# Leaky relu of a graph attention layer: linear part by VectorE from PSUM instead of by a matmul

## The chip, the cores and the metric

One Trainium2 chip, one core. The metric is the device time of one execution in microseconds; the time shown for the kernel before is the median of three runs. The three layers share one program, launched once.

## What is computed

A small network on a graph of 3125 nodes with 32 features and 100000 edges (sorted by destination): an edge MLP, two graph convolutions, and then three attention layers (GATv2, 8 heads of 32 channels), with a layer norm behind each of the four. Only the attention layers matter here:

```python
xl = (x @ Wl).reshape(-1, H, C)
xr = (x @ Wr).reshape(-1, H, C)
e = jax.nn.leaky_relu(xl[src] + xr[dst], 0.2)
logits = jnp.einsum('ehc,hc->eh', e, att)
m = jax.ops.segment_max(logits, dst, num_segments=N_NODES)
p = jnp.exp(logits - m[dst])
denom = jax.ops.segment_sum(p, dst, num_segments=N_NODES)
alpha = p / denom[dst]
out = jax.ops.segment_sum(alpha[:, :, None] * xl[src], dst, num_segments=N_NODES)
return out.mean(axis=1) + bias
```

Since leaky_relu(z) = 0.2 z + 0.8 relu(z), its sum with `att` can be made in two parts: a linear one, straight from the rows x of an edge's two nodes, and one from relu(z).

## The kernel before, in words

Edges lie in slots of 128, one edge to a partition; 8 slots make one step g (512 columns by 2 sides), there are G = 104 steps a layer, and 8 steps make a chunk. A loop over u = 0 to G + LAG - 1 (LAG = 10) runs on every engine, each with its own written-out list of instructions in fixed order; semaphores tie them. In step u the rows of step u are turned into logits, while step k = u - 10 is weighted and summed into `acc`.

- GpSimd, `pool_gathers` (L340): 8 indirect DMAs for each g, fetching table rows into one of two `rows` buffers. It waits until TensorE (`x_made`) and ScalarE (`xs_kept`) are done with g - 2.
- TensorE, `pe_attention`: `z_half(u,0)` (L848) multiplies the turned rows `xT` by `wcat` into two PSUM banks Z; `sums_half(k,0)` (L877) sums weighted rows; `linear(u)` (L856) adds the linear part of the logits into bank LG by way of `linblk`; `z_half(u,1)` writes the same two banks Z once more; `logits_half(u,0)` (L865) multiplies relu(z) by `attblk`; `rows_in(u+1)` (L833, L836) turns the next rows; `sums_half(k,1)`; `logits_half(u,1)`. Before `z_half` it waits on `rz_made`, since the banks must have been read.
- ScalarE, `act_attention`: `leaky(g,t)` (L573) makes relu(z) of two banks into `rz`; further it copies rows and logits, and takes exponentials.
- VectorE, `attention(l)`: `weigh(k,side)` (L1432), weights times rows, 1056 elements, one operand in PSUM; `add(k,side)` (L1442), twice, into `acc` at a window read from a register. At a chunk's end, where phase = u % 8: phase 0 has two scans (L1445, L1449) and `exchange` (L1457 to L1470), whose result TensorE turns (L920) before it ends the step; phase 1 has `settle`, with two scans again, `lasts`, `fall`; phase 2 has `fscale` (L1037), which waits for a small matmul of TensorE (L894), and a scaling of `acc` (L1498) ahead of all else. VectorE works through its list strictly in order.

The weights' preparation stands in the first convolution's setup (L1374 to L1382): `linblk` and the last columns of `wcat` are made there by products with `att`, reduces and copies.

The wait that the change touches most, on TensorE:

```python
def z_half(g, t):
    pe.wait_ge(xt_ready, l * G + g + 1)
    pe.wait_ge(rz_made, 4 * (l * G + g) + 2 * t)
```

Of the kernel before, what the change touches and what calls it, by code (L numbers as in the profile page):

```python
# [17 lines left out]
ALU = mybir.AluOpType  # L18
# [7 lines left out]
P = 128  # L26
# [42 lines left out]
def build(nc, x, edge_blocks, L0, W_gcn, b_gcn, gat, out):  # L69
    with ExitStack() as ctx:  # L70
# [58 lines left out]
        linblk = [sb(f"linblk{l}", [P, 7 * H + P]) for l in range(LAYERS)]  # L129
# [123 lines left out]
        rz_made, l_summed, lg_copied = sem("rz_made"), sem("l_summed"), sem("lg_copied")  # L253
# [305 lines left out]
        def act_attention(act, l):  # L559
# [8 lines left out]
            def leaky(g, t):  # L568
# [3 lines left out]
                for side in range(2):  # L572
                    act.activation(rz[:, 2 * t + side, :], ps[:, Z + side, :], ACT.Relu).then_inc(rz_made, 1)  # L573
# [66 lines left out]
        def _(act):  # L640
            act.wait_ge(weights_zeroed, 2 + 3 * LAYERS)
# [179 lines left out]
        def pe_attention(pe, l):  # L821
# [21 lines left out]
            def z_half(g, t):  # L843
                pe.wait_ge(xt_ready, l * G + g + 1)
                pe.wait_ge(rz_made, 4 * (l * G + g) + 2 * t)
# [5 lines left out]
            def linear(g):  # L851

                n = g % 8
                if n == 0:
                    pe.wait_ge(lg_copied, l * CHUNKS + g // 8)
                pe.matmul(ps[:, LG, :], linblk[l][:, (7 - n) * H:(7 - n) * H + P], xT[:, g % 2, :],  # L856
                          start=(n == 0), stop=False, skip_group_check=True)

            def logits_half(g, t):
                n = g % 8  # L860
                pe.wait_ge(rz_made, 4 * (l * G + g) + 2 * t + 2)
                for side in range(2):
# [3 lines left out]
                              start=False, stop=(n % 4 == 3 and t == 1), skip_group_check=True).then_inc(l_summed, 1)  # L866
# [16 lines left out]
            for u in range(G + LAG):  # L883
# [11 lines left out]
                if u < G:  # L895
                    linear(u)
                    z_half(u, 1)
                    logits_half(u, 0)
# [125 lines left out]
        def _(v):  # L1024
# [80 lines left out]
            for t in [w1[:, :], w2[:, :, :]] + [w[:, :, :] for w in wcat] + [w[:, :, :] for w in attblk] + [w[:, :] for w in linblk]:  # L1105
                v.memset(t, 0.0).then_inc(weights_zeroed, 1)
# [111 lines left out]
            for l in range(LAYERS):  # L1218
                ts(attblk[l][:, :, 3 * H:4 * H], attblk[l][:, :, 3 * H:4 * H], 0.8, None, ALU.mult)
# [149 lines left out]
            tmp2 = T2f[:, 0:2 * HC].rearrange("p (k c) -> p k c", k=2)  # L1369
            tmp = T2f[0:C, 2 * HC:3 * HC]  # L1370
            for l in range(LAYERS):


                stt(tmp2, wcat[l][:, :, 0:HC], 0.2, down(attrow[l][:, :], 2), ALU.mult, ALU.mult)  # L1374
                for k in range(2):
                    link(v.tensor_reduce(wcat[l][:, k, HC:ZC], tmp2[:, k, :].rearrange("p (h c) -> p h c", h=H),
                                         AX.X, ALU.add))
# [258 lines left out]
```

## Time and profile before

| | |
|---|---|
| median of 3 runs | 6472.8 us (6467.22 to 6487.99) |
| the profiled execution's own time | 6470.45 us |
| its span | 6468.7 us |
| mean granted TensorE clock | 0.92 |
| busy: TensorE, weight load | 84%, 55% |
| busy: GpSimd, VectorE, ScalarE | 65%, 50%, 30% |

Busy time is the time in which an engine had an instruction running, as a share of the span. TensorE's matmuls are pipelined, and one float32 matmul of the program is two records (so `z_half`, two matmuls, is x4); from the start of one to the start of the next instruction is the better measure of what it costs. The three attention loops lie at 2767 to 3904, 4006 to 5150 and 5252 to 6392 us.

### The profile page before, as it was taken

Reading aid. Unit: us, or ns where it says so; the run is one execution under the profiler, and the core shown is the slowest. Engines: PE = TensorE matmul, PEld = TensorE weight load, DVE = VectorE, ACT = ScalarE, POOL = GpSimd, SP = SyncE. Lnnn points to the kernel's source line nnn. Section 1 sums busy time; section 2 is a strip of 40 time slices with the busy share of each in tenths; the row PEclk is TensorE's granted clock in tenths of the full one; section 3 lists DMA queues with packets and bytes.
Section 4 is the critical chain, followed back from the end, with each engine's and each line's share of the span. In section 5 each row is a group of like instructions: output and inputs, shape, how many; then the busy total and the mean of one; then the engine's idle time right before and its main releaser. Section 6 shows DMA issues by size and latency. Waiting matters only on the chain.

```text
span 6468.7 us, 138175 instructions
## 1 busy us (share of the span) xinstructions
PE 5462.8 (84%) x47565; PEld 3535.7 (55%) x47565; DVE 3216.3 (50%) x5767; ACT 1959.8 (30%) x3916; POOL 4227.3 (65%) x4383
## 2 busy tenths in 40 slices
PE   1888888868886888689999986899999679999995
PEld 1666666667775777535455544354444444455553
DVE  8222323266567555535555555355555624555555
ACT  0333334345551000033333321333333123333330
POOL 0777777657775777477777742777777147777770
PEclk8899989879997999789999996999999879999997
DMA  1444444323332332234444431444444224444441
GB/s 36 113 114 113 113 113 113 102 72 83 78 83 66 83 83 77 54 87 119 117 121 121 120 94 38 104 120 117 121 121 118 65 56 116 120 119 121 119 117 32
DMA packets 645340, 626.97 MB, mean 97 GB/s; under 512 B 366244, under 2 KB 447915, under 8 KB 644779
## 3 DMA queue, kind: packets, MB, share of 16 engines
q1 hardware_dynamic: 498218, 437.16, 22.1%
q0 software_dynamic: 140352, 181.29, 14.6%
q8 instruction: 312, 5.11, 0.3%
q10 hardware_dynamic: 6208, 1.37, 0.1%
q14 instruction: 250, 2.04, 0.1%
HBM read 530.77 MB, written 88.55 MB: 96 GB/s over the span
## 4 chain that ended last, share of the span: by engine, by line
PE 40%; POOL 29%; issue 15%; DVE 9%; ACT 2%; DMA 2%; DVEq 1%; POOLq 0%
POOL rows L340 29%; PE ps L761 11%; PE ps L877 10%; PE ps L848 4%; PE ps L776 4%; PE ps L865 2%; PE ps L856 2%; DMA rows<-table,idx 2%; DVE region L1326 1%; DVE acc L1442 1%; PE ps L947 1%; PE ps L833 1%; PE ps L788 1%; DVE region L1034 1%; PE ps L963 1%
## 5 line engine op out<-in xcount | busy, mean ns | idle before, releaser
L340 POOL DMA_INDIRECT rows<-table,idx x3328 | 3231.9, 971 | 1556.8 <-issue 1108.3
L877 PE MATMUL ps<-region,hot 128*128 128x272 f32 x4992 | 1320.0, 408 | 92.2 <-DVE acc L1442 87.9
L877 PEld LDWEIGHTS ps<-region,hot 128*128 128x128 f32 x4992 | 910.9, 192 | 507.9 <-issue 335.8
L573 ACT ACTIVATE region<-ps 128x512 f32<-128x512 f32 x1248 | 677.4, 595 | 1681.9 <-PE ps L848 1681.9
L1442 DVE TENSOR_TENSOR acc<-acc,ps 128x272 f32 x1248 | 545.2, 437 | 1195.6 <-PE ps L877 1088.5
L1432 DVE TENSOR_TENSOR region<-ps,region 128x1056 f32<-128x1056 f32 x624 | 781.7, 1253 | 64.8 <-issue 53.7
L761 PE MATMUL ps<-hot,region 128*128 128x192 bf16 (+1 forms) x7488 | 773.0, 266 | 13.2 <-issue 9.6
L848 PE MATMUL ps<-xT,wcat 64*128 64x512 f32 x2496 | 721.9, 655 | 7.4 <-ACT region L573 4.9
L761 PEld LDWEIGHTS ps<-hot,region 128*128 128x128 bf16 x7488 | 701.9, 105 | 40.8 <-issue 9.9
L352 POOL DMA_INDIRECT rows<-table,idx x528 | 502.6, 952 | 270.5 <-issue 160.3
L865 PE MATMUL ps<-region,attblk 128*32 128x512 f32 x2496 | 667.5, 614 | 0.0
L352 POOL DMA_INDIRECT region<-table,idx x512 | 487.2, 952 | 156.0 <-issue 156.0
L848 PEld LDWEIGHTS ps<-xT,wcat 64*128 64x128 f32 x2496 | 193.4, 189 | 463.8 <-issue 431.0
L1289 DVE TENSOR_TENSOR acc<-acc,ps 128x96 f32 (+1 forms) x832 | 252.2, 303 | 354.4 <-PE ps L788 127.5
L833 PEld LDWEIGHTS ps<-identb,rows 128*32 128x32 bf16 x7488 | 239.8, 97 | 270.5 <-issue 264.5
L833 PE MATMUL ps<-identb,rows 128*32 128x128 bf16 x7488 | 300.0, 223 | 93.1 <-DMA rows<-table,idx 89.4
L620 ACT ACTIVATE region<-iota,region 128x128 bf16<-128x128 f32 x832 | 254.2, 389 | 283.3 <-PE ps L796 270.9
L856 PE MATMUL ps<-xT,linblk 128*128 128x512 f32 x624 | 331.3, 613 | 0.0
L836 PE MATMUL ps<-turned,xwin 128*32 128x128 bf16 x7488 | 313.2, 223 | 0.0
L1231 DVE TENSOR_TENSOR region<-ps,b3row 128x512 f32<-128x512 f32 x104 | 71.9, 691 | 483.5 <-PE ps L725 483.5
L776 PE MATMUL ps<-region 128*128 128x224 f32 x1248 | 308.3, 371 | 0.0
L1309 DVE TENSOR_TENSOR region<-ps,gmask 128x448 f32<-128x448 f32 x312 | 193.8, 621 | 176.8 <-PE ps L761 176.0
(264 smaller groups left out, 5880.0 us busy)
## 6 DMA issues: line engine op xcount, KB each, us to landing
hot<-hot_dram SPq DMA_DIRECT2D x624, 256.0 KB
turned<-turned_dram SPq DMA_DIRECT2D x624, 128.0 KB
rows<-table,idx POOLq DMA_INDIRECT x3856
hot_dram<-hot SPq DMA_DIRECT2D x104, 512.0 KB
xwin<-table SPq DMA_DIRECT2D x1664, 24.0 KB
region<-hot_dram SPq DMA_DIRECT2D x78, 512.0 KB
turned_dram<-turned SPq DMA_DIRECT2D x104, 256.0 KB
region<-r_dram SPq DMA_DIRECT2D x78, 256.0 KB
```

Of the source, the lines that this page charges most:

```text
L340: pool.indirect_dma_start(rows[:, b, j, :], None, table, bass.IndirectOffsetOnAxis(ap=idx[:, s:s + 1], axis=0)).then_inc(gathered[b], 16)
L352: pool.indirect_dma_start(rows4[at % 4][:, j, :], None, table, bass.IndirectOffsetOnAxis(ap=idx[:, 8 * g + j:8 * g + j + 1], axis=0)).then ...
L573: act.activation(rz[:, 2 * t + side, :], ps[:, Z + side, :], ACT.Relu).then_inc(rz_made, 1)
L761: mm = pe.matmul(ps[:, GB + i % 2, 224 * j:224 * j + n], bt[b][:, k, at:at + P], tabparts[:, k::FOLD, (2 + s) * C:(3 + s) * C], start=(k = ...
L776: mm = pe.matmul(ps[:, DB[i % 2], 0:GROUPS * C], dhot[b][:, at, :], picked[b][:, at, :, :].rearrange("p g c -> p (g c)"), start=(j == 0), ...
L833: m1 = pe.matmul(ps[q:q + C, XT, j * P:(j + 1) * P], rowparts[b][:, at, 2 * C + s * C:2 * C + (s + 1) * C], identb[:, :], start=(s == 0), ...
L848: pe.matmul(ps[:, Z + side, :], wcat[l][q:q + 64, side, t * P:(t + 1) * P], xT[q:q + 64, g % 2, :], start=True, stop=True).then_inc(z_summ ...
L856: pe.matmul(ps[:, LG, :], linblk[l][:, (7 - n) * H:(7 - n) * H + P], xT[:, g % 2, :], start=(n == 0), stop=False, skip_group_check=True)
L865: pe.matmul(ps[q:q + 32, LG, :], attblk[l][:, t, p_:p_ + 4 * H], rz[:, 2 * t + side, :], start=False, stop=(n % 4 == 3 and t == 1), skip_g ...
L877: mm = pe.matmul(ps[:, AG + i, 0:PC + H], hot[:, b, 4 * side + 2 * i + j, :], px[b][:, 4 * side + 2 * i + j, :], start=(j == 0), stop=(j = ...
L1432: v.tensor_tensor(to, at.unsqueeze(3).broadcast_to([P, 4, H, HK]), xs[:, (k // 8) % 2, n, 4 * side:4 * side + 4, :].unsqueeze(2).broadcast ...
L1442: v.tensor_tensor(at, at, ps[:, AG + i, 0:PC + H], ALU.add).then_inc(att_added, 1)
```

## The change

The linear matmul, `linblk` and the preparation for both go. ScalarE's Relu now carries the factor 0.8 and counts on a semaphore of its own, `relu_made`. TensorE's `z_half` and `logits_half` wait for that. There are two of the new instructions in each of the 104 steps of each layer. The gathers stay as they are.

```diff
-        linblk = [sb(f"linblk{l}", [P, 7 * H + P]) for l in range(LAYERS)]
...
-                    act.activation(rz[:, 2 * t + side, :], ps[:, Z + side, :], ACT.Relu).then_inc(rz_made, 1)
+                    act.activation(rz[:, 2 * t + side, :], ps[:, Z + side, :], ACT.Relu, scale=0.8).then_inc(relu_made, 1)
...
             def z_half(g, t):
                 pe.wait_ge(xt_ready, l * G + g + 1)
-                pe.wait_ge(rz_made, 4 * (l * G + g) + 2 * t)
+                pe.wait_ge(rz_made, 2 * (l * G + g) + t)
...
-            def linear(g):
-
-                n = g % 8
-                if n == 0:
-                    pe.wait_ge(lg_copied, l * CHUNKS + g // 8)
-                pe.matmul(ps[:, LG, :], linblk[l][:, (7 - n) * H:(7 - n) * H + P], xT[:, g % 2, :],
-                          start=(n == 0), stop=False, skip_group_check=True)
-
             def logits_half(g, t):
                 n = g % 8
-                pe.wait_ge(rz_made, 4 * (l * G + g) + 2 * t + 2)
+                pe.wait_ge(rz_made, 2 * (l * G + g) + t + 1)
+                if n == 0 and t == 0:
+                    pe.wait_ge(lg_copied, l * CHUNKS + g // 8)
...
                 if u < G:
-                    linear(u)
                     z_half(u, 1)
...
-            for l in range(LAYERS):
-                ts(attblk[l][:, :, 3 * H:4 * H], attblk[l][:, :, 3 * H:4 * H], 0.8, None, ALU.mult)
...
-                stt(tmp2, wcat[l][:, :, 0:HC], 0.2, down(attrow[l][:, :], 2), ALU.mult, ALU.mult)
-                for k in range(2):
-                    link(v.tensor_reduce(wcat[l][:, k, HC:ZC], tmp2[:, k, :].rearrange("p (h c) -> p h c", h=H),
-                                         AX.X, ALU.add))
-                    cp(linblk[l][:, 7 * H + 64 * k:8 * H + 64 * k], wcat[l][:, k, HC:ZC])
...
+                def leaky(g, t):
+                    if g >= G:
+                        return
+                    v.wait_ge(relu_made, 4 * (l * G + g) + 2 * t + 2)
+                    to = rz[:, 2 * t:2 * t + 2, :]
+                    v.scalar_tensor_tensor(to, ps[:, Z:Z + 2, :], 0.2, to, ALU.mult, ALU.add).then_inc(rz_made, 1)
...
                     link(scan_ahead(c, carrycol[:, 0:1]))
+                    leaky(u, 0)
                     link(scan_back(c, carrycol[:, 1:2]))
...
                         if k + 1 >= 0 and k + 1 < G:
                             weigh(k + 1, 0)
+                        leaky(u, 0)
                         v.wait_ge(lg_copied, l * CHUNKS + c + 1)
...
                             weigh(k + 1, 1)
+                        leaky(u, 1)
                         exchange(c)
...
                         if windows:
                             add(k, 0, windows)
+                        leaky(u, 1)
                         v.wait_ge(fall_made, l * CHUNKS + c + 1)
...
                         if 0 <= k + 1 < G:
                             weigh(k + 1, 0)
+                        leaky(u, 0)
+                        if 0 <= k + 1 < G:
+                            weigh(k + 1, 1)
                         if windows:
                             add(k, 0, windows)
-                        if 0 <= k + 1 < G:
-                            weigh(k + 1, 1)
+                        leaky(u, 1)
                         if windows:
                             add(k, 1, windows)
```

How the instructions stand, at three places. In these rows `region` is one of three large buffers that hold `rz`, weights and scans; a scan is shown as SCALAR_TENSOR_TENSOR too, told by its line and by `newF` or `newR`.

VectorE, phase 0 of a chunk, before, from the first `weigh` to the second:

```order
L1432 TENSOR_TENSOR region<-ps,region 128x4x264
L1445 SCALAR_TENSOR_TENSOR region<-newF,region 128x512
L1449 SCALAR_TENSOR_TENSOR region<-newR,region 128x512
L1442 REGISTER_ALU
L1442 ISA
L1442 TENSOR_TENSOR acc<-acc,ps 128x272
L1442 REGISTER_ALU x2
L1442 ISA
L1442 TENSOR_TENSOR acc<-acc,ps 128x272
L1432 TENSOR_TENSOR region<-ps,region 128x4x264
```

The same place in the changed kernel, from behind the first `weigh` to the exchange's first copy (L1423 is `weigh`, L1413 the new `leaky`, L1436 and L1440 the scans, L1433 `add`, L1035 a copy):

```order
L1413 SCALAR_TENSOR_TENSOR region<-ps,region 128x1024
L1436 SCALAR_TENSOR_TENSOR region<-newF,region 128x512
L1440 SCALAR_TENSOR_TENSOR region<-newR,region 128x512
L1433 REGISTER_ALU
L1433 ISA
L1433 TENSOR_TENSOR acc<-acc,ps 128x272
L1433 REGISTER_ALU x2
L1433 ISA
L1433 TENSOR_TENSOR acc<-acc,ps 128x272
L1423 TENSOR_TENSOR region<-ps,region 128x4x264
L1413 SCALAR_TENSOR_TENSOR region<-ps,region 128x1024
L1035 COPY ahead<-ps 1x16x16
```

`leaky(u,0)` stands ahead of the scans, `leaky(u,1)` between the second `weigh` and the exchange.

VectorE, phase 2, before, from `fscale` on:

```order
L1037 TENSOR_SCALAR fscale<-ps,first_hot 128x8
L1421 TENSOR_LOAD packed
L1421 ISA x2
L1498 REGISTER_ALU
L1498 ISA
L1498 TENSOR_TENSOR acc<-acc,fscale 128x264
L1432 TENSOR_TENSOR region<-ps,region 128x4x264
```

and in the changed kernel:

```order
L1029 TENSOR_SCALAR fscale<-ps,first_hot 128x8
L1405 TENSOR_LOAD packed
L1405 ISA x2
L1490 REGISTER_ALU
L1490 ISA
L1490 TENSOR_TENSOR acc<-acc,fscale 128x264
L1423 TENSOR_TENSOR region<-ps,region 128x4x264
L1413 SCALAR_TENSOR_TENSOR region<-ps,region 128x1024
L1423 TENSOR_TENSOR region<-ps,region 128x4x264
L1433 TENSOR_TENSOR acc<-acc,ps 128x272
```

The new instruction stands behind `fscale`, the scaling of `acc` (L1490) and the first `weigh`; the second `weigh` is now ahead of the adds.

TensorE, the start of the same phase 2, before:

```order
L924 MATMUL ps<-ident,region 128x128 x4
L848 MATMUL ps<-xT,wcat 128x512 x2
L877 MATMUL ps<-region,hot 128x272 x4
L894 MATMUL ps<-fdiag,ones 128x8
L856 MATMUL ps<-xT,linblk 128x512
L848 MATMUL ps<-xT,wcat 128x512 x2
L865 MATMUL ps<-region,attblk 32x512 x2
```

and in the changed kernel (L847 `z_half`, L870 `sums_half`, L887 the small matmul, L858 `logits_half`):

```order
L916 MATMUL ps<-ident,region 128x128 x4
L847 MATMUL ps<-xT,wcat 128x512 x2
L870 MATMUL ps<-region,hot 128x272 x4
L887 MATMUL ps<-fdiag,ones 128x8
L847 MATMUL ps<-xT,wcat 128x512 x2
L858 MATMUL ps<-region,attblk 32x512 x2
```

The linear matmul between the small one and the second `z_half` is gone.

## Rows read from the trace of the kernel before

**Rows 1.** First loop: window, us, busy (x) of PE PEld DVE ACT POOL, clock, DMA.
```profile
2767.00:3904.00 1137.00, 1064.83 (x8686) 538.18 (x8686) 572.78 (x880) 361.96 (x781) 779.16 (x816) 0.98 0.43 111
```

**Rows 2.** The gathers' line in that loop: durations in ns, and waits.
```profile
L340 POOL DMA_INDIRECT rows<-table,idx x816: 938/944/1938, 2766.7 to 3808.5; - x164
...
  PE ps L836: 7.3, 2
```

**Rows 3.** TensorE in time order, ordinary step u = 22: start us, us, instruction.
```profile
2986.97 1.13 PE L848 MATMUL ps<-xT,wcat 64*128 64x512 f32 x4
...
2989.97 1.02 PE L856 MATMUL ps<-xT,linblk 128*128 128x512 f32 x2
2990.92 1.13 PE L848 MATMUL ps<-xT,wcat 64*128 64x512 f32 x4
...
2993.64 2.10 PE L877 MATMUL ps<-region,hot 128*128 128x272 f32 x8
...
2996.65 1.13 PE L848 MATMUL ps<-xT,wcat 64*128 64x512 f32 x4
```

**Rows 4.** ScalarE in time order, same step: the two Relus.
```profile
2988.18 1.08 ACT L573 ACTIVATE region<-ps 128x512 f32<-128x512 f32 x2 [3.29 <-PE ps L848]
```

**Rows 5.** A VectorE line in the convolutions, 1024 elements, one input in PSUM.
```profile
L1326 DVE TENSOR_TENSOR region<-dloc,ps x130: 1211/1214/1221, 1350.5 to 2673.8; 128x1024 bf16<-128x1024 f32 x130
```

**Rows 6.** VectorE in time order, steps u = 22 and 24 to 26.
```profile
2987.03 1.26 DVE L1432 TENSOR_TENSOR region<-ps,region 128x1056 f32<-128x1056 f32 x1 [0.23 <-issue]
...
3008.56 1.22 DVE L1445 TENSOR_TENSOR_SCAN region<-newF,region 128x512 f32<-128x512 bf16 x1
...
3012.08 1.25 DVE L1432 TENSOR_TENSOR region<-ps,region 128x1056 f32<-128x1056 f32 x1
3014.64 0.41 DVE L1043 COPY ahead<-ps 1x256 f32<-1x256 f32 x1 [1.31 <-PE ps L905]
...
3017.27 0.16 DVE L1043 COPY ahead<-state 1x8 f32<-1x8 f32 x1
...
3024.97 0.44 DVE L1442 TENSOR_TENSOR acc<-acc,ps 128x272 f32 x1 [0.36 <-DVE acc L1442]
...
3034.19 1.26 DVE L1432 TENSOR_TENSOR region<-ps,region 128x1056 f32<-128x1056 f32 x1
```

**Rows 7.** TensorE in time order: first `z_half` of steps 8, 24 to 27, 103; one `sums_half`.
```profile
2839.72 1.13 PE L848 MATMUL ps<-xT,wcat 64*128 64x512 f32 x4
...
3007.35 1.13 PE L848 MATMUL ps<-xT,wcat 64*128 64x512 f32 x4
...
3017.76 1.13 PE L848 MATMUL ps<-xT,wcat 64*128 64x512 f32 x4
...
3025.56 2.07 PE L877 MATMUL ps<-region,hot 128*128 128x272 f32 x8
...
3029.13 1.13 PE L848 MATMUL ps<-xT,wcat 64*128 64x512 f32 x4
...
3039.73 0.70 PE L848 MATMUL ps<-xT,wcat 64*128 64x512 f32 x2
...
3815.66 0.70 PE L848 MATMUL ps<-xT,wcat 64*128 64x512 f32 x2
```

**Rows 8.** A pause of TensorE in the third loop, and the granted clock behind it.
```profile
5408.55 0.22 PE L833 MATMUL ps<-identb,rows 128*32 128x128 bf16 x1 [1.87 <-DMA rows<-table,idx]
...
5409.33 3.56 PE L877 MATMUL ps<-region,hot 128*128 128x272 f32 x8
5412.83 0.80 PE L865 MATMUL ps<-region,attblk 128*32 128x512 f32 x2
...
5409.90:5413.20 3.30, 3.30 (x9) 1.88 (x9) 0.44 (x2) 0.22 (x1) 2.64 (x3) 0.50 0.20 37
```

**Rows 9.** GpSimd in time order: a gather beside a scan of phase 1.
```profile
3019.63 1.66 POOL L340 DMA_INDIRECT rows<-table,idx  x1 [0.30 <-issue]
```

**Rows 10.** A group of the setup that the change removes.
```profile
L1376 DVE TENSOR_REDUCE wcat<-T 128x8 f32<-128x256 f32 x6 | 2.5, 420 | 0.2
```

More of the change, by code:

```diff
@@ L252, in build @@
         x_made, xt_ready, xs_kept = sem("x_made"), sem("xt_ready"), sem("xs_kept")
-        rz_made, l_summed, lg_copied = sem("rz_made"), sem("l_summed"), sem("lg_copied")
+        rz_made, relu_made, l_summed, lg_copied = sem("rz_made"), sem("relu_made"), sem("l_summed"), sem("lg_copied")
         heads_made, tails_turned = sem("heads_made"), sem("tails_turned")
@@ L640, in _ @@
         def _(act):
-            act.wait_ge(weights_zeroed, 2 + 3 * LAYERS)
+            act.wait_ge(weights_zeroed, 2 + 2 * LAYERS)
             for dst, srcw in weights:
@@ L865, in logits_half @@
                     pe.matmul(ps[q:q + 32, LG, :], attblk[l][:, t, p_:p_ + 4 * H], rz[:, 2 * t + side, :],
-                              start=False, stop=(n % 4 == 3 and t == 1), skip_group_check=True).then_inc(l_summed, 1)
+                              start=(n % 4 == 0 and t == 0), stop=(n % 4 == 3 and t == 1), skip_group_check=True).then_inc(l_summed, 1)
             def sums_half(k, side):
@@ L1103, in add_steps @@
                         between[k]()
-            for t in [w1[:, :], w2[:, :, :]] + [w[:, :, :] for w in wcat] + [w[:, :, :] for w in attblk] + [w[:, :] for w in linblk]:
+            for t in [w1[:, :], w2[:, :, :]] + [w[:, :, :] for w in wcat] + [w[:, :, :] for w in attblk]:
                 v.memset(t, 0.0).then_inc(weights_zeroed, 1)
@@ L1368, in _ @@
             T2f = T2[:, :, :].rearrange("p w c -> p (w c)")
-            tmp2 = T2f[:, 0:2 * HC].rearrange("p (k c) -> p k c", k=2)
             tmp = T2f[0:C, 2 * HC:3 * HC]
             for l in range(LAYERS):
-                stt(tmp2, wcat[l][:, :, 0:HC], 0.2, down(attrow[l][:, :], 2), ALU.mult, ALU.mult)
-                for k in range(2):
-                    link(v.tensor_reduce(wcat[l][:, k, HC:ZC], tmp2[:, k, :].rearrange("p (h c) -> p h c", h=H),
-                                         AX.X, ALU.add))
-                    cp(linblk[l][:, 7 * H + 64 * k:8 * H + 64 * k], wcat[l][:, k, HC:ZC])
                 tt(wsum[l][:, 0:HC], wsum[l][:, 0:HC], wcat[l][0:C, 0, 0:HC], ALU.add)
@@ L1471, in exchange, with settle @@
                     v.sem_inc(carry_made, 1)
-                def settle(c):
+                def settle(c, u):
                     at = l * CHUNKS + c
@@ L1484, in settle @@
                     v.tensor_scalar(fall[:, :], fall[:, :], 0.0, first_old[0:H, c:c + 1], ALU.min, ALU.mult).then_inc(e_made, 1)
-                for u in range(8, G + LAG):
+                for u in range(G + LAG):
                     phase, c, k = u % 8, u // 8 - 1, u - LAG
@@ L1489, in attention @@
                     if phase == 1 and ends:
-                        settle(c)
+                        settle(c, u)
                     if phase == 2 and ends and c > 0:
```

## The prediction

> **What bounds the kernel now.** The page first: TensorE 84% busy, GpSimd 65%, VectorE 50%. Such shares are means over stages, so the second view is the stretch of one attention layer's loop, the only place (with a short setup) that the change touches. There TensorE is busy for 1064.8 of 1137 us and GpSimd for 779.2, VectorE for 572.8 [rows 1], and one would say that TensorE bounds the loop and that a matmul less must help. The third view, the gather's own line, speaks against it: its 816 gathers run from 2766.7 to 3808.5, which is 10.2 us for each step of eight, and of all that time GpSimd waited 7.3 us for TensorE [rows 2]. So the gathers hold the loop, and TensorE keeps up with a little to spare. How little is read from its timeline: an ordinary step goes from 2986.97 to 2996.65, 9.68 us [rows 3]. The three steps at a chunk's end, where VectorE's scans and the exchange lie between TensorE's parts, take longer: phase 0 from 3007.35 to 3017.76 is 10.41, phase 1 to 3029.13 is 11.37, phase 2 to 3039.73 is 10.60 [rows 7]. Eight steps of TensorE's own chain are 5 x 9.68 + 32.38 = 80.8 us, while eight steps in truth take 82.2 (from u = 8 at 2839.72 to u = 103 at 3815.66 are 95 steps in 975.9 us, 10.27 each [rows 7]). The chain has 1.4 us in 82 to spare: less cannot be gained there, since every gather stays, and a chain that grows by more is paid in full.
>
> **What is removed.** The linear matmul holds TensorE from 2989.97 to 2990.92, 0.95 us a step [rows 3]. By itself that would shorten a chain that does not bound: worth nothing but at the loop's last step. In the setup the products, the six reduces (0.42 each [rows 10]) and the copies of `linblk` go; with products and small copies I put the piece at 2.0 us a layer, 6 us in all. TensorE waits for VectorE there, so the 6 us are gained (lower end 0).
>
> **What is added, ordinary step.** Two new VectorE instructions, 1024 elements from PSUM and SBUF. The nearest row, 1024 elements with one PSUM input, took 1.21 us, and the `weigh` with 1056 took 1.26 [rows 5, 6]; I take 1.22. 312 x 2 x 1.22 = 761 us of VectorE time, and it has room: the question is what waits. Times are from the start of `z_half(u,0)`. The Relu runs from 1.21 to 2.29 [rows 4]. The second `z_half` used to need only that, and came at 3.95 after sums and linear [rows 3]; now it also needs `leaky(u,0)`. VectorE is free (its `weigh` ran 0.06 to 1.32 [rows 6]). With 0.10 for the handover from ScalarE (no row shows it; between 0 and the 0.15 that VectorE to TensorE takes, 3025.41 to 3025.56 [rows 6, 7]) it runs 2.39 to 3.61, and `z_half(u,1)` starts at 3.76. Without linear TensorE was ready at 3.00, so it idles 0.76. From there to the next step are 5.73 us as before (2990.92 to 2996.65), and `leaky(u,1)`, done some 3.76 later, is hidden behind rows and sums. The step: 3.76 + 5.73 = **9.49**, 0.19 less than now. Four fifths of the saved matmul are lost to the wait.
>
> **Phase 0.** The scans began 1.21 into the step [rows 6]; they now stand behind `leaky(u,0)` and begin at 3.54 (successive instructions overlap by some 0.07), a shift of 2.33. The second `weigh` ended at 5.98, now at 8.31. Then `leaky(u,1)`, to 9.45, and only then the exchange, which used to begin at 7.29 and takes 2.79 (3014.64 to 3017.43 [rows 6]). It ends at 12.17. TensorE needs its result before it ends the step, 0.33 later: **12.50** instead of 10.41.
>
> **Phase 1.** `settle` has `leaky(u,0)` between its two scans: all behind it comes 1.14 later, the second `add` ends at 7.65 + 1.14 = 8.79 [rows 6]. `sums_half(k,1)` waits for it, and so it did before, so the whole 1.14 shows: 11.37 becomes **12.51**.
>
> **Phase 2** is where the order hurts most. `fscale` and the scaling of `acc` wait for a matmul and stand first, then the `weigh` from 5.06 to 6.32 [rows 6], then `leaky(u,0)`: 6.24 to 7.46. `z_half(u,1)` is ready near 3.4 and starts at 7.61, and 5.73 follow: **13.34** instead of 10.60. TensorE pauses some 4 us.
>
> **The sum.** Eight steps: 5 x 9.49 + 12.50 + 12.51 + 13.34 = 85.8 us against 82.2. The gathers (two buffers of rows) no longer decide. Over the 95 steps: 12 x 12.50 + 12 x 12.51 + 11 x 13.34 (the first chunk has no `fscale`) + 60 x 9.49 = 1016, against 975.9: +40.3 a layer. *The clock:* at 5408.55 TensorE had paused 1.87 us; behind it the granted clock was 0.50, the 1.2 GHz level, for 3.3 us, and a `sums_half` that takes 2.03 to the next instruction took 3.50 [rows 3, 8]. The pause of 4 us in phase 2 should do this each time, and TensorE is the chain just then: 11 x 1.6 = +17.6 a layer (ends 0 and three times that). *The tail:* in six steps behind the last row step both `weigh` now stand ahead of the adds; between 0 and 1.25 us each, I take 0.87 since TensorE has nothing else left there, 5.2, less one linear 0.95: +4.3. Three layers: 3 x (40.3 + 17.6 + 4.3) = 186.6, less 6 for the setup: **+181 us**. Against the profiled execution's 6470.45 this is 6651; the median of the runs shown, 6472.8, is 2 us above that execution, which changes nothing at this size.
>
> **A rule against the change, on the gathers.** The rows: a gather beside the scan of phase 1, two SBUF inputs, took 1.66 us instead of the median 0.944 [rows 2, 9]; yet with two `weigh` in each step (one input in PSUM) the median stays there. `leaky` has one PSUM input too, so I add nothing. The Trainium skill, page "SBUF — State Buffer", section "SBUF: two separate sides", says that a VectorE instruction in a two-port mode or with two SBUF inputs can lock GpSimd out of the port pair they share, and warns that this starves gathers issued by GpSimd. By its exact wording `leaky` is exempt; by its warning taken broadly the third rival below would come out.
>
> **The rivals.**
> 1. *The clock does not fall.* For it: over the loop the mean is 0.98 [rows 1], pauses and all. Then 6651 - 53 = **6598**.
> 2. *The clock falls more.* Phase 0 has a pause too, about 1.7 us before the exchange's end, and a pause of 4 us could cost twice. 3 x (17.6 + 12 x 1.6) = +110: **6761**.
> 3. *Gathers are held up by `leaky`.* Each for its 1.22: 8 gathers then take 9.99 + 2.44 = 12.4 us, 2.2 above 10.27, over 312 steps +675: some **7140**. The `weigh` rows speak against it.
> 4. *The other side: not slower.* The gathers stay the bound, because VectorE reaches its `leaky` sooner in the three chunk-end steps than I lay out (its adds and `weigh` overlapping the waits). The point that decides: eight steps of the chain at or under 82.2 us, so the three may lose only 2.4 together where I have 6.0. Then only the setup is gained: 6470 - 6 = **6464**. Against it: three separate places, each with the order fixed in one in-order queue.
>
> **How the numbers follow.** Forecast 0.50, clock does not fall 0.22, clock falls more 0.18, not slower 0.06, gathers held up 0.04. A measurement of this kernel tells about 0.3% (19 us) from no change. The predicted time is the likeliest case, 6651. The range, 6570 to 6785, takes in rivals 1 and 2 and, at its ends, the handover, the tail's and the setup's bounds (some 25 us together); it leaves out rivals 3 and 4. Slower by over 0.3%: 0.93; within 0.3%: 0.05; faster by over 0.3%: 0.02, if a chain with slack also clears waits that I do not see.
>
> **What would show it.** In the profile of the changed kernel: the new VectorE line x624 at 1.22 us; `z_half(u,0)` to the next in ordinary steps 9.5, in the three phases 12.5, 12.5 and 13.3; TensorE waiting for the new line before `z_half`, the longest in phase 2, near 4 us; the granted clock at 0.50 behind it; GpSimd waiting for TensorE's row matmuls by tens of us a layer where it had 7.3; the gathers still at 0.944. The forecast is wrong if GpSimd still issues without pause through the loops (rival 4), if gathers are longer (rival 3), or if the steps come out as laid out and the clock stays at 1.00 (rival 1).

## The result, and the profile after

The changed kernel takes 6716.8 us (median of 4 runs, 6710.9 to 6719.5) where the kernel before, run beside it, takes 6470.5 (4 runs, 6467.2 to 6488.0). The ratio is 1.0374, with a 95% interval of 1.0353 to 1.0394: slower, by 246 us. The prediction had 6651, with a range of 6570 to 6785.

The spans of the two profiled executions are 6709.2 and 6468.7 us, so 240.5 us have to be found. The page of the changed kernel, its span, its engines and two groups of instructions (the groups' last column is idle time before them):

```profile
span 6709.2 us, 137605 instructions
...
PE 5282.8 (79%) x46941; PEld 3451.5 (51%) x46941; DVE 3941.1 (59%) x6370; ACT 1957.0 (29%) x3916; POOL 4237.7 (63%) x4383
...
L847 PE MATMUL ps<-xT,wcat 64*128 64x512 f32 x2496 | 754.6, 679 | 371.1 <-DVE region L1413 368.0
L1413 DVE SCALAR_TENSOR_TENSOR region<-ps,region 128x1024 f32<-128x1024 f32 x624 | 763.4, 1223 | 442.0 <-ACT region L572 417.7
```

The new VectorE line is L1413, `leaky`, 624 times at 1.22 us. TensorE waited 368 us for it before `z_half` (now L847), more than the whole difference. Which part of these waits costs time must be read stage by stage. First the loop of the first layer, as a window and as the gathers' line (L339; columns as in [rows 1, 2]):

```profile
2767.00:3990.00 1223.00, 1011.03 (x8474) 517.11 (x8474) 817.67 (x1091) 359.54 (x778) 779.10 (x813) 0.94 0.40 103
```

```profile
L339 POOL DMA_INDIRECT rows<-table,idx x816: 938/944/1839, 2763.2 to 3875.6; - x164
...
  PE ps L832: 70.8, 13
```

The gathers themselves are what they were, 938/944 [rows 2], but the same 816 now end 67 us later, and GpSimd waits 70.8 us for TensorE where it waited 7.3. So the gathers hold the loop no longer; TensorE's chain does. The granted clock over this window is 0.94, where it was 0.98 over the shorter loop before [rows 1].

Where the 240.5 us lie, from the starts of the first `z_half` of steps 0, 8 and 103 in each of the three loops:

| stretch, three layers together | before | after | predicted | measured |
|---|---|---|---|---|
| everything ahead of the first loop | 2767.1 | 2763.6 | -6 | -3.5 |
| step 0 to step 8 | 222.7 | 251.3 | 0 | +28.6 |
| step 8 to step 103 | 2927.9 | 3119.5 | +174 | +191.6 |
| step 103 to the next loop or the end | 551.0 | 574.6 | +13 | +23.6 |

"Ahead of the first loop" is less sure than its figure: the other traces, from chips of the same pace, of kernels with the old setup have 2763.2 to 2769.2 there, those with the changed setup 2762.3 to 2772.3, so the 3.5 us are within what one execution differs from another.

TensorE in time order, steps 31 to 35 of the first layer (start, duration, line, and in brackets the pause before and what ended it). `z_half` is L847, `sums_half` L870:

```profile
3096.88 1.13 PE L847 MATMUL ps<-xT,wcat 64*128 64x512 f32 x4
3100.57 1.13 PE L847 MATMUL ps<-xT,wcat 64*128 64x512 f32 x4 [0.53 <-DVE region L1413]
3106.30 1.13 PE L847 MATMUL ps<-xT,wcat 64*128 64x512 f32 x4
...
3118.52 0.28 PE L912 MATMUL ps<-ident,staterow 1*128 1x1 f32 x2 [1.75 <-DVEq L1462]
3118.73 1.13 PE L847 MATMUL ps<-xT,wcat 64*128 64x512 f32 x4
3120.28 3.63 PE L870 MATMUL ps<-region,hot 128*128 128x272 f32 x8 [0.41 <-DVE acc L1433]
...
3131.24 1.13 PE L847 MATMUL ps<-xT,wcat 64*128 64x512 f32 x4
3132.33 2.07 PE L870 MATMUL ps<-region,hot 128*128 128x272 f32 x8
3134.33 0.38 PE L887 MATMUL ps<-fdiag,ones 8*128 8x8 f32 x2
3138.84 2.08 PE L847 MATMUL ps<-xT,wcat 64*128 64x512 f32 x4 [4.12 <-DVE region L1413]
...
3146.99 0.70 PE L847 MATMUL ps<-xT,wcat 64*128 64x512 f32 x2
```

An ordinary step is 9.42 us (3096.88 to 3106.30); phase 0 is 12.43 (to 3118.73), phase 1 12.51 (to 3131.24), phase 2 15.75 (to 3146.99). In phase 2 the second `z_half` starts 7.60 us after the first, behind a pause of 4.12, and it takes 2.08 instead of 1.13. VectorE in that phase shows what it waited for:

```profile
3134.75 0.23 DVE L1029 TENSOR_SCALAR fscale<-ps,first_hot 128x8 f32<-128x8 f32 x1 [2.49 <-PE ps L887]
3135.83 0.43 DVE L1490 TENSOR_TENSOR acc<-acc,fscale 128x264 f32 x1 [0.85 <-DVE fscale L1029]
3136.30 1.26 DVE L1423 TENSOR_TENSOR region<-ps,region 128x1056 f32<-128x1056 f32 x1
3137.48 1.22 DVE L1413 SCALAR_TENSOR_TENSOR region<-ps,region 128x1024 f32<-128x1024 f32 x1
```

`leaky` had nothing to wait for but its place: VectorE idled 2.49 us for `fscale`, did the scaling and a `weigh`, and only then came to it. The granted clock in two windows, the pause and what follows (columns as in [rows 1], the clock third from the end):

```profile
3134.70:3138.80 4.10, 0.01 (x1) 0.00 (x0) 3.16 (x5) 0.00 (x0) 2.18 (x3) 0.79 0.40 100
3138.80:3143.50 4.70, 4.66 (x50) 1.82 (x52) 3.06 (x4) 1.39 (x3) 0.00 (x0) 0.50 0.01 3
```

It falls to 0.50, the 1.2 GHz level, inside the pause and stays there over the next 4.7 us of TensorE's work. In the three loops of this trace 33 pauses of 4.1 us or a little more lie at that place behind step 8. With 9 of them the clock was at 0.50 for 3.4 us and the phase took 14.7 to 15.0 us; with 24 it was there for 6.8 us, the end of the pause included, and the phase took 15.6 to 16.6.

The start of the loop was put at nothing. TensorE, then VectorE, then GpSimd there:

```profile
2777.51 2.08 PE L847 MATMUL ps<-xT,wcat 64*128 64x512 f32 x4 [11.82 <-DVE region L1413]
```

```profile
2761.23 6.81 DVE L1539 TENSOR_REDUCE hot<-region 128x200 f32<-128x6400 f32 x1
...
2770.03 5.72 DVE L1545 MEMSET acc<- 128x6800 f32 x1 [1.59 <-issue]
...
2776.14 1.22 DVE L1413 SCALAR_TENSOR_TENSOR region<-ps,region 128x1024 f32<-128x1024 f32 x1
```

```profile
2782.86 0.94 POOL L339 DMA_INDIRECT rows<-table,idx  x1 [9.86 <-PE ps L832]
```

TensorE had turned the rows and begun the first `z_half` at 2763.62. The second needs `leaky(0,0)`, which stands in VectorE's list behind the self loops' reduce and the clearing of `acc`, 12.5 us of work that nothing in the first steps used to wait for: VectorE's own part of the loop began only at u = 8. The `rows` buffers stay taken, and GpSimd stands for 9.86 us.

### The profile page after: what moved, and what is told of

It is laid out like the page before. It is cut to its first block, busy times and chain, and to the rows that moved or that the text cites. A ratio compares the mean times of both kernels' runs of the same rounds, so it can differ in the third digit from the quotient of the medians.

```text
span 6709.2 us, 137605 instructions
## 1 busy us (share of the span) xinstructions
PE 5282.8 (79%) x46941; PEld 3451.5 (51%) x46941; DVE 3941.1 (59%) x6370; ACT 1957.0 (29%) x3916; POOL 4237.7 (63%) x4383
## 3 DMA queue, kind: packets, MB, share of 16 engines
q14 instruction: 254, 2.08, 0.1%
## 4 chain that ended last, share of the span: by engine, by line
PE 45%; DVE 19%; POOL 16%; issue 14%; ACT 2%; DVEq 1%; DMA 0%; POOLq 0%
POOL rows L339 16%; PE ps L760 11%; PE ps L870 10%; PE ps L847 8%; DVE region L1413 5%; PE ps L858 5%; PE ps L775 4%; DVE acc L1433 2%; ACT region L572 2%; PE ps L832 2%; PE ps L835 1%; DVE region L1436 1%; DVE region L1316 1%; PE ps L787 1%; PE ps L939 1%
## 5 line engine op out<-in xcount | busy, mean ns | idle before, releaser
L339 POOL DMA_INDIRECT rows<-table,idx x3328 | 3243.3, 975 | 1780.1 <-issue 1102.3
L870 PE MATMUL ps<-region,hot 128*128 128x272 f32 x4992 | 1351.8, 415 | 135.1 <-DVE acc L1433 132.1
L870 PEld LDWEIGHTS ps<-region,hot 128*128 128x128 f32 x4992 | 926.8, 196 | 574.0 <-issue 395.4
L847 PE MATMUL ps<-xT,wcat 64*128 64x512 f32 x2496 | 754.6, 679 | 371.1 <-DVE region L1413 368.0
L1413 DVE SCALAR_TENSOR_TENSOR region<-ps,region 128x1024 f32<-128x1024 f32 x624 | 763.4, 1223 | 442.0 <-ACT region L572 417.7
L1433 DVE TENSOR_TENSOR acc<-acc,ps 128x272 f32 x1248 | 542.8, 435 | 559.6 <-PE ps L870 376.6
L1423 DVE TENSOR_TENSOR region<-ps,region 128x1056 f32<-128x1056 f32 x624 | 779.0, 1252 | 56.4 <-issue 53.6
L858 PE MATMUL ps<-region,attblk 128*32 128x512 f32 x2496 | 703.6, 644 | 8.9 <-DVE region L1413 4.7
L847 PEld LDWEIGHTS ps<-xT,wcat 64*128 64x128 f32 x2496 | 206.2, 194 | 709.7 <-issue 685.7
L832 PE MATMUL ps<-identb,rows 128*32 128x128 bf16 x7488 | 350.6, 232 | 20.6 <-DMA rows<-table,idx 18.0
L832 PEld LDWEIGHTS ps<-identb,rows 128*32 128x32 bf16 x7488 | 268.7, 102 | 172.7 <-issue 168.2
L835 PE MATMUL ps<-turned,xwin 128*32 128x128 bf16 x7488 | 347.0, 230 | 0.0
L835 PEld LDWEIGHTS ps<-turned,xwin 128*32 128x32 bf16 x7488 | 256.8, 97 | 84.3 <-issue 84.1
```

The lines of the kernel that those rows point to most:

```text
L339: pool.indirect_dma_start(rows[:, b, j, :], None, table, bass.IndirectOffsetOnAxis(ap=idx[:, s:s + 1], axis=0)).then_inc(gathered[b], 16)
L832: m1 = pe.matmul(ps[q:q + C, XT, j * P:(j + 1) * P], rowparts[b][:, at, 2 * C + s * C:2 * C + (s + 1) * C], identb[:, :], start=(s == 0), ...
L835: m2 = pe.matmul(ps[q + C:q + 2 * C, XT, j * P:(j + 1) * P], xwin[:, b, 2 * side + j // 2, s * C:(s + 1) * C], turned[:, b, at * P:(at + 1 ...
L847: pe.matmul(ps[:, Z + side, :], wcat[l][q:q + 64, side, t * P:(t + 1) * P], xT[q:q + 64, g % 2, :], start=True, stop=True).then_inc(z_summ ...
L858: pe.matmul(ps[q:q + 32, LG, :], attblk[l][:, t, p_:p_ + 4 * H], rz[:, 2 * t + side, :], start=(n % 4 == 0 and t == 0), stop=(n % 4 == 3 a ...
L870: mm = pe.matmul(ps[:, AG + i, 0:PC + H], hot[:, b, 4 * side + 2 * i + j, :], px[b][:, 4 * side + 2 * i + j, :], start=(j == 0), stop=(j = ...
```

## The experiments

Four theories come from this. **A**: TensorE's chain bounds now, and the loss is the fixed order of VectorE's list: when it comes to `leaky`, and to what now stands behind `leaky`. **B**: VectorE's 763 us of new work are the loss, wherever they stand. **C**: much of it is the clock behind the pause in phase 2. **D**: the start is a loss of its own. And one theory on the kernel before, that the gathers bounded it. Every edit is to the changed kernel unless said otherwise. "Body" is step 8 to step 103, before 976 and after 1040 us a layer.

### The kernel before, without its linear matmul

This kernel leaves out the linear part of the logits; the first logits matmul of a sum then starts the bank afresh.

```diff
-                pe.matmul(ps[:, LG, :], linblk[l][:, (7 - n) * H:(7 - n) * H + P], xT[:, g % 2, :],
-                          start=(n == 0), stop=False, skip_group_check=True)
```

> The kernel before with the linear matmul left out and nothing in its place, so the linear part of the logits is missing from the result. Theory: the gathers bound the loops, so the matmul was worth nothing but one at each loop's end: 6470 less some 3 us, ratio 0.998 to 1.001, ordinary steps 9.99 us behind gathers at 1.249 us each. Rival, TensorE bounds the loops: 312 x 0.95 = 296 us less, 6175 us, ratio 0.954.

Measured: 6474.2 against 6469.4, ratio 1.0009 (0.9999 to 1.0019). The gathers' line over the first loop:

```profile
L340 POOL DMA_INDIRECT rows<-table,idx x825: 938/945/1903, 2764.9 to 3989.5; - x165
...
who waited for it (us, times):
  PE ps L833: 79.8, 60
```

A matmul of 0.95 us less in each of 312 steps, some 296 us of TensorE's time, is worth nothing. Phase 3, just behind a chunk's end, took 8.82 us instead of 9.67; then TensorE had caught up and phases 4 to 7 took 9.8 to 10.1 (medians), waiting 80 to 88 us a layer for rows. The body stayed at 973 to 978. The gathers bounded the kernel before.

### `leaky` first in phase 2

Two places change: `leaky(u,0)` goes ahead of the wait for `fscale`, and the first add goes ahead of the second `weigh` again, as in the kernel before.

```diff
+                    first = phase == 2 and ends and c > 0
+                    if first:
+                        leaky(u, 0)
                     if phase == 2 and ends and c > 0:
                         v.wait_ge(fall_spread, l * (CHUNKS - 1) + c)
...
-                        leaky(u, 0)
+                        if first:
+                            add(k, 0, windows)
+                        else:
+                            leaky(u, 0)
                         if 0 <= k + 1 < G:
                             weigh(k + 1, 1)
-                        if windows:
+                        if windows and not first:
                             add(k, 0, windows)
```

> The changed kernel with one edit, in phase 2: leaky(u,0) stands ahead of the wait for fscale, and the adds ahead of the second weigh. Theory (the order in VectorE's queue makes the wait): z_half(u,1) starts at 3.7 instead of 7.6 us, the sums then wait a little for the adds, the step falls from 15.75 to about 11.0 us, 33 of them: 157 us less, about 6560 us, ratio to before 1.014; the granted clock no longer falls there. Rival, VectorE's added load as such is the cost: the time moves to another place and the total stays within 20 us of 6717.

Measured: 6547.8, ratio 1.0120 (1.0103 to 1.0137), 169 us less than the changed kernel. TensorE's phase 2, then the start of VectorE's:

```profile
3129.77 1.13 PE L847 MATMUL ps<-xT,wcat 64*128 64x512 f32 x4
...
3133.46 1.13 PE L847 MATMUL ps<-xT,wcat 64*128 64x512 f32 x4 [0.21 <-DVE region L1413]
...
3140.57 1.13 PE L847 MATMUL ps<-xT,wcat 64*128 64x512 f32 x4
```

```profile
3132.09 1.23 DVE L1413 SCALAR_TENSOR_TENSOR region<-ps,region 128x1024 f32<-128x1024 f32 x1 [1.30 <-ACT region L572]
3133.28 0.23 DVE L1029 TENSOR_SCALAR fscale<-ps,first_hot 128x8 f32<-128x8 f32 x1
```

The pause is gone, `z_half` is back at 1.13, phase 2 takes 10.80, and the body 988 us. VectorE does exactly as much as in the changed kernel. Seven tenths of the loss were the places of two instructions in a list, which is theory A and C together; B as the whole cause is out. This run doesn't show how much of it is the second `weigh`'s place; the two versions with unawaited reduces below differ in that place too, and have 13.02 and 11.85 us for phase 2.

### The pause filled with useless matmuls

```diff
+                    for m in range(20):
+                        pe.transpose(ps[:, XT, 0:P], weight[:, 0:P], ident[:, :])
```

behind the small matmul that `fscale` waits for. Nothing is sooner; only the clock can differ.

> The changed kernel with 20 small matmuls of no use put into TensorE's pause of phase 2 (into the bank of the turned rows, free then), nothing else. Theory: z_half(u,1) still starts near 7.6 us, since VectorE decides that, but the granted clock stays at 2.4 GHz and the rest of the step takes 5.73 instead of 8.1 us: phase 2 falls from 15.75 to 13.3, 33 x 2.4 = 80 us less, about 6637 us, ratio to before 1.026. Rival, the extra 2.4 us are not the clock's but waits: no gain, 6717 or more.

Measured: 6632.8, ratio 1.0258 (1.0240 to 1.0275), 84 us less. TensorE's phase 2, and the clock behind it:

```profile
3133.78 1.13 PE L847 MATMUL ps<-xT,wcat 64*128 64x512 f32 x4
...
3137.19 2.40 PE L889 MATMUL ps<-ident,region 128*128 128x128 f32 x20
3141.38 1.13 PE L847 MATMUL ps<-xT,wcat 64*128 64x512 f32 x4 [1.79 <-DVE region L1415]
...
3147.10 1.13 PE L847 MATMUL ps<-xT,wcat 64*128 64x512 f32 x4
```

```profile
3142.00:3147.10 5.10, 5.10 (x68) 2.49 (x64) 3.28 (x6) 1.99 (x4) 1.89 (x2) 1.00 0.04 8
```

The second `z_half` still starts 7.60 after the first, as in the changed kernel, but the clock is at 1.00 and the rest of the step takes 5.72 where it took 8.15. Phase 2 is 13.32 instead of 15.75. This is theory C alone, measured: 2.4 us for a pause by the phase's median, and 84 us for the 36 of them (12 a layer, one in the tail). In the traces the bodies are 80 us shorter and the tails 13, while the stretch ahead of the loops came out 6 longer, which is scatter. TensorE is busier and the kernel faster.

The Trainium skill, page "TensorE: Matmul & The Clock Gate", section "HAM oscillation — how this bites in real kernels", describes this pattern, pauses in a loop that put the clock down for the work that follows. The trace of the changed kernel agrees (0.50 with each of the 33 pauses of 4.1 us), and here the pause is a wait on VectorE instead of on a DMA.

### The start in pieces

The self loops' reduce and the clearing of `acc` are cut into four pieces of windows, `start_piece(n)`, issued by VectorE behind steps 0 to 3.

```diff
+                        link(v.tensor_reduce(selfsum[:, ws, :].rearrange("p w h -> p (w h)"),
+                                             prodself[:, ws, :].rearrange("p w (h c) -> p (w h) c", h=H), AX.X, ALU.add))
+                        link(v.memset(acc[:, ws, :], 0.0))
...
+                    start_piece(u)
```

> The changed kernel with one edit: the reduce of 6.8 us and the memset of 5.7 us that stand ahead of VectorE's loop are cut into four pieces and done behind the leaky of steps 0 to 3. Theory: the first leaky no longer waits for them, the first z_half(u,1) loses its pause of 11.8 us, the third group's gathers start some 9.5 us sooner: 3 x 9.5 = 28 us less, about 6689 us, ratio to before 1.034. Rival, the gathers catch up anyway because the loop behind is not held by them: the start of each loop is paid by the chain, so the same 28; if instead nothing moves, the loop's end is set elsewhere, 6717.

Measured: 6685.4, ratio 1.0338 (1.0321 to 1.0355), 31 us less. The second `z_half`, which stood for 11.82 us:

```profile
2769.18 2.08 PE L847 MATMUL ps<-xT,wcat 64*128 64x512 f32 x4 [2.64 <-DVE region L1413]
```

Step 0 to step 8 takes 76.4 us a layer instead of 83.8, 22 us in three layers of the 28.6 that were lost there; the other 9 us of the gain lie in bodies and tails, and no run says why. The body stays at 1038. Theory D holds, and its loss adds to the others.

### VectorE's work, without anyone waiting for it

To the kernel before, which keeps its linear matmul and the wait on ScalarE's Relu alone, reduces of 1.21 us are added on VectorE in the places of `leaky`. Nobody waits for their result. In the first version the second `weigh` also stands ahead of the adds, as in the changed kernel:

```diff
+                def load():
+                    link(v.tensor_reduce(spare[:, :], ones[:, :].unsqueeze(1).broadcast_to([P, 8, P]), AX.X, ALU.add))
...
+                        load()
+                        if 0 <= k + 1 < G:
+                            weigh(k + 1, 1)
                         if windows:
                             add(k, 0, windows)
-                        if 0 <= k + 1 < G:
-                            weigh(k + 1, 1)
+                        load()
```

> The kernel before, its linear matmul kept, with one more VectorE instruction of about 1.15 us (a reduce of constants that nobody reads) at each of the places where the changed kernel has a leaky: 624 of them, and TensorE waits for none. Theory (the loss comes from waits on the chain more than from VectorE's load): ordinary steps stay as they are, the three steps at a chunk's end grow by 1.0 to 1.15 us each since scans, adds and exchange come later, eight steps 84.1 instead of 82.2 us: about +68 us, 6540, ratio 1.0105, at most 1.015. Rival, the load itself is the cost: as much as the change, ratio 1.03 or more.

Measured: 6681.2, ratio 1.0327 (1.0312 to 1.0342), a miss: this is the rival's number, not the theory's. Where it lies: the bodies lose 129 us of these 210, the tails 71. The reduces also stood in the ten steps of the tail, where the changed kernel has no `leaky`, which made each tail 22 to 25 us longer. In the bodies phases 0, 1 and 2 took 11.34, 12.63 and 13.02, ordinary steps 9.67 as before. So with the changed kernel's order of VectorE's list two thirds of its bodies' loss of 192 us come without anyone waiting for the new instructions, by what stands behind them: adds, scans and the exchange, for which TensorE had waited all along. The next version has no reduce for u >= G and the adds where the kernel before has them. The chip that it ran on first was slower in everything.

> The run with the unawaited reduces again, with its two flaws mended: no reduce in the ten steps behind the last group (the changed kernel has no leaky there; they cost 22 us a layer), and the second weigh back behind the adds as in the kernel before. Expected from the rows of the run before: phase 0 stays at 11.3 and phase 1 at 12.6 us; in phase 2 the adds come one reduce later, 10.60 becomes about 11.75 us; ordinary steps 9.67. Eight steps 84.1 against the gathers' 82.2: about 22 us a layer, 67 us in all, ratio 1.010 (1.006 to 1.014). If the load itself, wherever it stands, is the cost: 1.02 or more.

Measured there: 8469.3 against 8421.1 for the kernel before, ratio 1.0055 (1.0037 to 1.0074). On a chip like the others':

> The same kernel as the run on unawaited reduces without those in the tail, for the same reason. On a chip as in the first jobs: eight steps 84.1 us, about +67 us, ratio 1.010 (1.006 to 1.014). If VectorE's load itself is the cost: 1.02 or more.

Measured: 6551.9 against 6469.6, ratio 1.0127 (1.0111 to 1.0142), 82 us. VectorE's reduces over the whole span:

```profile
L1428 DVE TENSOR_REDUCE spare<-ones x576: 1193/1210/1221, 2775.7 to 6388.5; 128x8 f32<-128x1024 f32 x192
```

576 of them, none in the first eight steps of a layer. Ordinary steps keep their 9.67 us, but phases 0, 1 and 2 take 11.34, 12.63 and 11.85 where they took 10.6, 11.4 and 10.6, and the body is 1003 us. So 698 us of VectorE's time cost 82. The price is paid at chunk ends, where VectorE itself lies on the chain, and it is about a third of what the change costs.

### All orders mended

The start in pieces; in phase 0 the first scan ahead of `leaky(u,0)`; in phase 1 the adds of the step right behind the subtraction in `settle`; in the tail the adds ahead of the second `weigh`; in phase 2 both `weigh`, then `leaky(u,0)`, ahead of `fscale`. The last of these:

```diff
+                    first = phase == 2 and ends and c > 0
...
+                    if first:
+                        if 0 <= k + 1 < G:
+                            weigh(k + 1, 0)
+                            weigh(k + 1, 1)
+                        leaky(u, 0)
```

> The changed kernel with VectorE's order mended at all places: the start as in the run on the start, in phase 0 the first scan ahead of leaky(u,0), in phase 1 the adds right behind the subtraction, in phase 2 both weighs and leaky(u,0) ahead of fscale and the adds ahead of leaky(u,1), in the last steps the adds ahead of the second weigh. Theory: phases about 11.3, 11.2 and 9.6 us, eight steps of the chain 79.2 us, under the gathers' 82.2, so the gathers bind again: before less the setup, 6465 us (6455 to 6490), ratio 0.997 to 1.003. Rival, VectorE's 763 us more are a cost that no order hides: above 6550 us.

Measured: 6476.2 against 6471.5, ratio 1.0011 (1.0002 to 1.0019). Phase 2 missed what was expected of it, 9.6: the two `weigh`, with one of the step before, kept `leaky(u,0)` from starting until 4.17 us into the step, and TensorE paused 2.05 us. By itself that made the phase 11.25 us, in 11 of 27 cases; in the other 16 the clock fell behind the pause, and it took 12.7 to 12.9. One case of each kind, the second `z_half` and the clock behind its start:

```profile
3030.11 2.08 PE L847 MATMUL ps<-xT,wcat 64*128 64x512 f32 x4 [2.05 <-DVE region L1413]
...
3112.82 1.13 PE L847 MATMUL ps<-xT,wcat 64*128 64x512 f32 x4 [2.06 <-DVE region L1413]
```

```profile
3030.10:3033.30 3.20, 3.19 (x14) 0.85 (x16) 1.30 (x3) 1.07 (x3) 2.00 (x3) 0.50 0.07 13
3112.80:3116.00 3.20, 3.18 (x58) 1.66 (x59) 1.95 (x5) 1.39 (x3) 2.59 (x3) 1.00 0.26 54
```

The next version puts both `weigh` behind `leaky(u,0)`:

```diff
                     if first:
-                        if 0 <= k + 1 < G:
-                            weigh(k + 1, 0)
-                            weigh(k + 1, 1)
                         leaky(u, 0)
...
+                        if 0 <= k + 1 < G and first:
+                            weigh(k + 1, 0)
...
+                        if 0 <= k + 1 < G and first:
+                            weigh(k + 1, 1)
```

> The changed kernel with all orders mended as in the run on all orders, but phase 2 in another order: leaky(u,0), fscale, the scaling, the adds, the first weigh, leaky(u,1), the second weigh, the adds. There phase 2 took 12.0 us, since three weighs stood ahead of leaky(u,0). Theory: phase 2 about 9.6 us, eight steps of the chain 79 us, gathers bind with room to spare: the loop's 95 steps back to 976 us (980 to 985 in the run on all orders), with the setup's 3.5 us and some 4 us a layer at the loops' ends gained as there: 6455 us, ratio 0.997 to 0.999. Rival, VectorE's load slows the gathers or the chain in some other way: no better than 1.001.

Measured on the slower chip: 8339.2 against 8421.1, ratio 0.9893 (0.9878 to 0.9909). A piece of the first loop there:

```profile
3792.00:5060.00 1268.00, 1007.49 (x7758) 518.12 (x7758) 722.65 (x976) 324.15 (x713) 721.38 (x751) 0.91 0.37 91
```

The same matmuls and gathers as in 982 us elsewhere (below) take 1268 us here, and the DMA moves 91 GB/s instead of 118, which is the same bytes in the longer time and so no cause. The gathers' issue is as short as ever (0.945), but GpSimd waits 219 us for ScalarE and 92 for TensorE in this window. The part ahead of the loops, which the change hardly touches, takes 3700 us instead of 2770. Why this chip is slower the runs don't settle; what they say is that in this kernel on it the issue of gathers does not decide alone, and that there the mended kernel wins by 1.1%. No trace of the kernel before was kept from this chip, so where these 82 us lie stays open. On a chip like the others':

> The same kernel as the run on the best orders, since in that job the kernel before itself took 8421 us where it took 6470 in the others. If the chip is as in the first jobs: 6455 us, ratio 0.997 to 0.999, phase 2 about 9.6 us, 95 steps 976 us a layer. If it is again at 8400 us, the ratio repeats 0.989.

Measured: 6467.5 against 6469.6, ratio 0.9992 (0.9983 to 1.0001). TensorE's phase 2, a window of the loop, and its gathers:

```profile
3119.93 1.13 PE L847 MATMUL ps<-xT,wcat 64*128 64x512 f32 x4
...
3129.57 1.13 PE L847 MATMUL ps<-xT,wcat 64*128 64x512 f32 x4
```

```profile
2846.00:3828.00 982.00, 878.57 (x7760) 447.88 (x7760) 723.45 (x977) 335.06 (x713) 729.37 (x757) 0.99 0.46 118
```

```profile
L339 POOL DMA_INDIRECT rows<-table,idx x818: 942/947/1702, 2762.6 to 3820.4; - x164
...
  PE ps L835: 7.1, 1
```

Phase 2 is 9.64 (expected 9.6), eight steps of the chain about 79 us, and the clock 0.99. GpSimd again waits 7.1 us for TensorE, as in [rows 2], and the body is 977 to 982. All 246 us are gone by order alone, the start's two instructions cut into pieces for it, with the change's arithmetic left as it is. Nor is anything gained: the gathers bound it again, as they bounded the kernel before.

## Why the prediction was right, and where its terms were off

- **What bounds the kernel before, and that the removed matmul is worth nothing:** right, and shown by taking it away (1.0009).
- **Ordinary step 9.49:** measured 9.42. The second `z_half` starts at 3.69 instead of 3.76, since the handover from ScalarE, put at 0.10, took 0.03 (Relu to 3099.17, `leaky` from 3099.20); the 5.73 behind it stand. The pause is 0.53 by the row, which counts from the modelled end of `sums_half`; counted as in the prediction it is 0.69 where 0.76 was worked out.
- **Phase 0 12.50, phase 1 12.51:** measured 12.43 and 12.51.
- **Phase 2, second `z_half` at 7.61, pause some 4 us:** measured 7.60 and 4.12. With the clock held up the phase takes 13.32, where 13.34 was laid out.
- **+40.3 a layer for the body without the clock:** the run with the filled pause, the changed kernel without the clock's loss in phase 2, has a body of 1013.1 in the mean, +37.1.
- **The clock term, mis-sized:** 1.6 us a pause was taken from [rows 8], a pause of 1.87 with 3.3 us at 0.50 behind it. Where the pause of 4.1 also had 3.4 us at 0.50 behind it, the phase lost 14.8 - 13.3 = 1.5, as taken; but 24 of 33 pauses had 6.8, and the mean is 2.4: 80 us over the bodies instead of 53. The pause of phase 0, feared in the second rival, is 1.75 us; behind 11 of 29 such pauses 3.4 us at 0.50 followed (the `sums_half` of 3.63 us at 3120.28 is one), yet phase 1, where this slow work lies, still took 12.5: TensorE's pause of 1.26 before the second `sums_half`, a wait for VectorE's adds, took up the delay (0.3 us of it are left in most cases).
- **The start, the step that failed.** The prediction let everything outside the 95 steps and the tail cost nothing. `leaky(0,0)` in fact stands behind 12.5 us of setup work on VectorE, and TensorE stood 11.82 us: +28.6 us in three layers. Cutting it up took 22 us out of this stretch and 31 off the kernel. The rows of VectorE ahead of the loop were not read.
- **The tail, mis-sized:** +4.3 a layer was predicted, 7.9 measured. The adds behind two `weigh` were right: a plain step of the tail goes from 5.91 to 6.74 us, +0.83 for the 0.87 taken. But the tail also holds a phase 2 (u = 106) with its pause; the filled pause made the tail shorter by 4.2 us a layer.
- **The setup, not shown:** 6 us were taken; the two traces differ by 3.5, and traces with the same setup differ by up to 10.
- **The rivals:** the clock does fall (first, out). It falls more than forecast (second), which is 27 of its 110 us. The gathers' median stays 0.944 beside 624 `leaky` (third, out). More sharply: the 795 gathers of the changed kernel that ran in part beside `leaky` and beside no scan took 0.938 to 0.957, and all but one of the 59 over 1.1 us ran beside a scan, as all 44 in the kernel before did. By the exact wording of the Trainium skill, page "SBUF — State Buffer", section "SBUF: two separate sides", a VectorE instruction with one input in PSUM, and in no two-port mode, leaves the shared port pair free; these gathers agree. The point that decides the fourth, three chunk-end steps within 2.4 us of before, is what the mended orders reach: with them the kernel is not slower.

Off were thus the start (28.6), the clock (27), the tail (10.7) and the stretch ahead of the loops (2.5), less 9 for steps that came out shorter; with the 5.9 us by which the median of the runs lies above the profiled execution, this is the 66 us between 6651 and 6716.8. The result stayed within the range because the range had been carried to the second rival, for a clock loss of which a quarter came. That this room also held the start is luck.

## What to carry to other kernels

When an instruction that others wait for moves to an engine with a fixed list, its duration is the small part of its price: read for each stage what stands ahead of it there, the stages outside the steady loop (start and tail) first, because an order that cost nothing while nobody waited becomes part of the chain with the first waiter. Read also what now comes later behind the new instruction: here that alone cost 82 us with one order of the list and 210 with another. A pause on TensorE can be paid twice, once as itself and once as slow work behind it (here always with 4.1 us, in 16 of 27 cases with 2.05), so a filled pause was cheaper than an empty one, and no pause was best. Before an engine is relieved, show by leaving its work out that it bounds anything: here 296 us of matmuls were worth 0.

## What the runs showed of the hardware

- The stretch at the lower clock came as 3.4 or as 6.8 us, with pauses of the same 4.1 us at the same place in the program. Of 27 pauses of 2.05 us in phase 2 (both `weigh` ahead of `leaky`), 16 were followed by a stretch of 3.4 us and 11 by none; of 29 pauses of 1.75 us in phase 0 of the changed kernel, 11 and 18.
- A gather beside a scan took up to 1.92 us where the median is 0.944; beside `leaky`, which reads one input from PSUM, and beside no scan, it took 0.957 or less (both in the changed kernel).
- Useless work can make a kernel faster: 20 transposes in each of 36 pauses took 84 us off.
- One chip ran the kernel before at 8421 us that others ran at 6470, and the mended kernel was slower there both ahead of the loops (3700 against 2770 us) and in them (1268 against 982). The ratios were others too: 0.9893 for the version that is 0.9992 elsewhere, 1.0055 for the one that is 1.0127. A ratio near one belongs to the chip that it was measured on.
